# Taking two evicted blocks apart with two VectorE instructions instead of four, in a graph network kernel

## What is computed

```python
def _L0_gnn_ref(node_feats, edge_feats, src, dst, W_e, b_e, eps, W1, b1, gamma, beta, W2, b2):
    e = edge_feats @ W_e + b_e
    m = jax.nn.relu(e + node_feats[src])
    agg = jax.ops.segment_sum(m, dst, num_segments=n)
    h = agg + (1.0 + eps) * node_feats
    z = h @ W1 + b1
    ...                                  # batch norm, relu
    return z @ W2 + b2

def gcn_layer(h, W, b):                  # three of them, each with relu
    hw = h @ W
    msg = hw[src] * norm[:, None]        # norm from the degrees, self loops included
    return jax.ops.segment_sum(msg, dst, num_segments=n) + b

x = _layernorm(x + _L0_gnn_ref(x, ...))
x = _layernorm(x + _L1_gnn_ref(x, ...))
```

## Time and profile before

| | |
|---|---|
| runs | 3148.88, 3151.97, 3140.8 us (median 3148.88) |
| profiled execution | 3141.62 us, of which the span from first to last instruction is 3139.8 us |
| TensorE busy | 2557.4 us (81%), granted clock 0.825 of full speed over the span |
| VectorE busy | 2149.1 us (68%) |
| GpSimd busy | 1605.2 us (51%) |
| ScalarE busy | 968.6 us (31%) |

### The profile page before, as it was taken

One profiled execution on the slowest core, in us unless ns is written; L12 is line 12 of the kernel. 1 busy time (PEld: TensorE's weight loads), 2 busy tenths in 40 slices (PEclk: granted clock), 3 DMA queues, 4 the chain that ended last, 5 costly groups with the idle time before them and its releaser, 6 DMA issues.

```text
span 3139.8 us, 48219 instructions
## 1 busy us (share of the span) xinstructions
PE 2557.4 (81%) x16328; PEld 2238.1 (71%) x16328; DVE 2149.1 (68%) x4255; ACT 968.6 (31%) x1165; POOL 1605.2 (51%) x1582
## 2 busy tenths in 40 slices
PE   4767878777778777777778787787899999999995
PEld 4667767677667766767677776666788888888884
DVE  8767677776767676767676777765798854454446
ACT  1112222222222222222222222226555554455441
POOL 7777777777777777777777777740000000000000
PEclk9687777877777777777776777778999999999997
DMA  6444444444444444444444444432334323323332
GB/s 218 113 120 122 125 124 126 119 125 123 124 124 123 126 123 126 123 125 123 125 124 123 123 124 122 126 98 78 124 121 161 141 107 135 157 105 140 141 141 83
DMA packets 145379, 394.65 MB, mean 126 GB/s; under 512 B 36821, under 2 KB 100096, under 8 KB 139760
## 3 DMA queue, kind: packets, MB, share of 16 engines
q1 hardware_dynamic: 93298, 278.01, 24.6%
q0 software_dynamic: 50176, 102.50, 15.3%
q10 hardware_dynamic: 1662, 10.97, 0.9%
HBM read 286.56 MB, written 104.77 MB: 125 GB/s over the span
## 4 chain that ended last, share of the span: by engine, by line
POOL 48%; PE 30%; issue 15%; DVE 3%; ACT 2%; DMA 1%; DVEq 0%; SPq 0%; ACTq 0%
POOL work L662 48%; PE psE L958 13%; PE psA L958 13%; PE psA L929 1%; PE psA L901 1%; PE psS L890 1%; PE psE L823 1%; ACT wide L767 0%; PE psA L851 0%; PE psS L837 0%; DVE z L1200 0%; PE psE L885 0%; DMA work<-in_x_flat,idx 0%; ACT xn L740 0%; PE psA L885 0%
## 5 line engine op out<-in xcount | busy, mean ns | idle before, releaser
L662 POOL DMA_INDIRECT work<-in_x_flat,idx x1568 | 1598.0, 1019 | 485.7 <-issue 476.5
L823 PE MATMUL psE<-we,work 65*128 65x128 f32 x3136 | 594.4, 367 | 471.1 <-DVE work L1086 426.6
L823 PEld LDWEIGHTS psE<-we,work 65*128 65x128 f32 x3136 | 548.2, 271 | 491.0 <-DMA work<-in_edge_cols 377.6
L1086 DVE TENSOR_TENSOR work<-psE,work 128x1024 f32<-128x1024 f32 x196 | 239.9, 1224 | 557.4 <-DMA work<-in_x_flat,idx 556.7
L851 PE MATMUL psA<-z 128*128 128x245 bf16 x3136 | 582.7, 354 | 0.0
L1106 DVE TENSOR_SCALAR z<-iota_c,key,scale 128x490 bf16<-128x490 f16 x1568 | 555.1, 415 | 21.6 <-DVE z L1098 0.9
L700 ACT ACTIVATE work<-psA 128x490 int32 x392 | 227.3, 580 | 903.9 <-PE psA L851 887.6
L958 PE MATMUL psE<-wide,halves 128*128 128x500 f32 (+1 forms) x2058 | 447.9, 375 | 5.7 <-ACT halves L776 5.3
L837 PEld LDWEIGHTS psS<-onehot,work 128*128 128x128 f32 x3136 | 417.1, 214 | 38.5 <-issue 32.8
L837 PE MATMUL psS<-onehot,work 128*128 128x72 f32 x3136 | 419.6, 292 | 21.2 <-DVE acc L1118 21.2
L687 ACT ACTIVATE work<-work 128x1024 f32<-128x1024 f32 x196 | 207.2, 1057 | 733.7 <-DVE work L1086 733.6
(11 more groups left out here) (160 smaller groups left out, 1330.1 us busy)
## 6 DMA issues: line engine op xcount, KB each, us to landing
counts<-adjacency SPq DMA_DIRECT2D x36, 3062.5 KB, 9.9
adjacency<-work SPq DMA_DIRECT2D x392, 245.0 KB
work<-in_edge_cols SPq DMA_DIRECT2D x196, 256.0 KB
work<-in_x_flat,idx POOLq DMA_INDIRECT x1568
counts<-adjacency SPq DMA_DIRECT2D x3, 1592.5 KB, 6.2
acc<-in_x_cols ACTq DMA_DIRECT2D x1, 3136.0 KB, 23.2
xn<-in_x_rows ACTq DMA_DIRECT2D x1, 3136.0 KB, 32.0
x_spill<-xn SPq DMA_DIRECT2D x12, 256.0 KB, 2.3
```

Of the source, the lines that this page charges most:

```text
L662: gp.indirect_dma_start(gath[0:size(g), g % R, j, :], None, x_flat[:, :], bass.IndirectOffsetOnAxis(ap=idx[0:size(g), g, j:j + 1], axis=0) ...
L823: mm = pe.matmul(psE0[0:n, j, :], eaT[0:FE + 1, g % RE, j, 0:n], we[:, :], start=True, stop=True)
L1086: ve.tensor_tensor(gath[0:n, g % R, :, :], psE0[0:n, :, :], gath[0:n, g % R, :, :], ALU.add).then_inc(sum_ok, 1)
```

## The change

Four changes go together. VectorE takes both banks of a step apart with two instructions on 980 values each, where it used four on 490. Both stand behind `add_window`; the first bank's used to stand ahead of `low_hots`. The semaphore that releases the stored blocks to SyncE, and the buffers to ScalarE, now rises by two after the second instruction. There are four stored blocks instead of three, and the work area grows by 490 words a partition.

```diff
-SLOTS = 3
+SLOTS = 4
...
-        work = sb("work", [P, 9574])
+        work = sb("work", [P, 10064])
...
-            def take_apart(w):
-                ve.wait_ge(evac_ok, w + 1)
+            def take_apart(s):
+                w = HQ * s
+                ve.wait_ge(evac_ok, w + HQ)
                 if w >= SLOTS:
-                    ve.wait_ge(stored[w % SLOTS], 16 * (w // SLOTS))
-                to, fro = full[:, w % SLOTS, :, :, :], taken_low[:, w % TAKEN, :, :]
+                    for i in range(HQ):
+                        ve.wait_ge(stored[(w + i) % SLOTS], 16 * ((w + i) // SLOTS))
+                to = full[:, w % SLOTS:w % SLOTS + HQ, :, :, :].rearrange("p s b h n -> p (s b) h n")
+                fro = taken_low[:, w % TAKEN:w % TAKEN + HQ, :, :].rearrange("p s b n -> p (s b) n")
                 ve.tensor_scalar(to[:, :, 0, :], fro, NIBBLES, None, ALU.bitwise_and)
-                ve.tensor_scalar(to[:, :, 1, :], fro, 4, NIBBLES, ALU.logical_shift_right, ALU.bitwise_and).then_inc(apart_ok, 1)
+                ve.tensor_scalar(to[:, :, 1, :], fro, 4, NIBBLES, ALU.logical_shift_right, ALU.bitwise_and).then_inc(apart_ok, HQ)
...
                     window_hot(s + 1)
-                    if s >= 1:
-                        take_apart(2 * (s - 1))
                     low_hots(s + 1)
...
                 add_window(s, at)
                 if s >= 1:
-                    if s + 1 == G:
-                        take_apart(2 * (s - 1))
-                    take_apart(2 * (s - 1) + 1)
+                    take_apart(s - 1)
...
-            for m in range(2 * (G - 1), 2 * G):
-                take_apart(m)
+            take_apart(G - 1)
```

More of the change, by code:

```diff
@@ L183, in build @@
         taken_low = taken.bitcast(U16).rearrange("p s (b n two) -> p s b n two", b=2, two=2)[:, :, :, :, 0]
-        assert taken_at + TAKEN * 2 * HC <= 9574 and RB * HC + LB * J * P // 2 <= 10112
+        assert taken_at + TAKEN * 2 * HC <= 10064 and RB * HC + LB * J * P // 2 <= 10112
         wide_at = dead_at
```

## The result

| | before | after |
|---|---|---|
| median | 3145.68 us (3138.53 to 3151.97, 13 runs) | 3156.13 us (3150.38 to 3161.58, 13 runs) |
| span of the profiled execution | 3139.8 us | 3156.1 us |
| VectorE busy | 2149.1 us, 4255 instructions | 2132.5 us, 3863 instructions |
| granted TensorE clock over the span | 0.825 | 0.822 |

The ratio is 1.0035, with a 95% interval from 1.0025 to 1.0045: the changed kernel is slower by 10.4 us. VectorE works 17 us less and the kernel takes longer. The forecast was 3,197 us, slower by 48 to 55. The direction was right and the size was not.

What follows compares the result with a forecast made beforehand. GpSimd's gather issues were taken as the bound; waits for VectorE would add 0.24 to 0.33 us a step, taken as 55 us on 3,141.6: 3,197 us. Likeliest case 3,165 to 3,225; 8 in 10 for 3,110 to 3,280.

Steps and rivals of the forecast that it cites:

- What bounds: Graph stage: eight GpSimd gather issues set a step of 10.51 us, 0.52 us of it waits caused by VectorE.
- No change: Rival: only VectorE's busy time moves and gathers lose 0.5 us as before; 3,142 to 3,149 us, chance 0.13.
- L: Time from the end of a group's last gather issue to T; forecast to fall from 3.3 towards 1.6 to 2.5 us.
- T: Start of the row addition L1086, from which all VectorE work of a step follows at fixed distances.
- The long pair's durations: The two VectorE instructions on 980 values: each 0.58 us of VectorE's time, 0.65 us from start to end.
- The wait at L1098 or L1092: Gather requests held by VectorE: at L = 1.8, 0.63 us at L1098 and 0.07 at the first long instruction.
- 0.12 (L1106): Gather request held until a running L1106 ends: 0.12 us a step at L = 1.6 and 2.5.
- 0.40 (second long instruction): Gather request held until the second 980-value instruction ends: 0.40 us a step at L = 1.6 and 2.5.
- the sum: Waits added per step: 10.75 us against 10.42 (regular) to 10.51 (mean), 46 to 64 us in 193 steps.
- one every 0.32: Spacing of the four L1106 in VectorE's step: ends from T + 4.19 to 5.16 before, 3.54 to 4.51 after.
- Longer waits: Rival: L rests at 1.6, requests wait longer, step 11.09 us, 120 us more in all: 3,262 us, chance 0.17.
- The port rule: VectorE in two-port mode and GpSimd share ports; first issuer keeps them, so twice the length waits up to twice as long.

Runs made afterwards that it cites:

- early load: The changed kernel with the edge load issued between the two stores instead of behind them: 3178.73 us, ratio 1.0114.
- the place alone: The kernel before with four stored blocks and four instructions on 490 values, both pairs behind the window addition: 3187.47 us, ratio 1.0134.
- the first order: The changed kernel with VectorE's step reordered, window addition first, then L1092, and no gap behind low_hots: 3352.11 us, ratio 1.0661.
- early pair: The changed kernel with its two 980-value instructions ahead of low_hots instead of behind the window addition (also called length): 3154.6 us, ratio 1.0019.
- slots: The kernel before with only the fourth stored block and the larger work area: 3148.29 us, ratio 0.9997.
- no gap: The changed kernel with TensorE instead of VectorE waiting for low_hots, removing 0.11 us of VectorE idle time behind it: 3269.37 us, ratio 1.0391.
- second order: The changed kernel with VectorE's step reordered, two L1106 and a long instruction first, add_window late, wait behind low_hots kept: 3223.19 us, ratio 1.0238.

## Why the prediction was right in sign and wrong in size

**What bounds: right.** GpSimd's issues bound before and after. VectorE's saving (17 us busy) found no place in the chain, and "No change" by unchanged waits is not what happened either.

**L: right.** "L falls from 3.3 towards 1.6 to 2.5": 1.65. The stores were forecast at T + 6.33 and 8.6 to 9.6, the load at 9.0 to 10.0; they leave at T + 6.4, 9.0 and 9.4 (medians). The early load shows the mechanism from the other side.

**The long pair's durations: nearly right.** 0.65 us forecast; L1117 takes 0.651, L1116 0.864. In the early place L1116 takes 0.676. Behind the window addition an issue has begun 0.6 us ahead of it (1009.36), and the same extra 0.2 us stood in the L1113 of 0.61 behind L1118 in the earlier trace rows: I had carried it into the distances, not into the duration. GpSimd seems to hold VectorE up there in turn; no run tested that.

**The wait at L1098 or L1092: right.** Forecast for L = 1.8 were 0.63 and 0.07; the median waits at L = 1.8 are 0.61 and 0.05. At the usual L of 1.65 they are 0.55 and 0.05.

**The step that failed: what else is held up.** The prediction let a running L1106 hold a request until its end, and so added 0.12 (L1106) and with it 0.40 (second long instruction) at L = 1.6 and 2.5. These are not there. The longest wait of a request met by each instruction, from all issues of the traces of before, after, the place alone and the first order (requests that were passed over, below, left out):

| instruction | length us | longest wait us |
|---|---|---|
| L1106 (490 values) | 0.40 | 0.13 |
| L1113, L1114 (490 values) | 0.40 | 0.26 |
| L1116, L1117 (980 values) | 0.65 | 0.47 |
| L1092 | 0.75 | 0.59 |
| L1098 | 1.22 | 1.07 |
| L1086, L1118 or L1121 | 1.23, 0.29 | 0 |

L1106 holds a request up only in its last 0.13 us. But that alone doesn't take the 0.12 away. The request came at T + 4.39, just where the sum had it, and the sum had the fourth L1106 end at T + 4.51, 0.12 later. In the steps with L = 1.6 that end is at T + 4.7 and the third L1106's at T + 4.38. The second L1106, behind a request let in at T + 3.14, lasts 0.61 us there, and 0.5 in most other steps, where the earlier trace rows had already shown four L1106 in 1.45 us and not in the 1.37 of "one every 0.32". So the request came 0.3 us ahead of an end, where an L1106 holds nobody: of the 170 requests that came at T + 4.2 to 4.5 in the changed kernel, 169 waited for nothing. Nor did the sum keep to its own rule: at L = 1.8 and 3.3 it has a request at T + 4.27 and charges nothing, though the fourth L1106 would be running.

The steps with L = 1.5 to 1.7 took 10.59 us (median), not 11.09, and those at 2.5 took 10.24, not 10.74. "Longer waits", at 3,262 us, rested on the same term. The 0.40 at L1117 hung on it too: only a request that an L1106 had delayed would have come late enough to be held up by L1117.

**The sum.** "0.24 to 0.33 us, in 193 steps 46 to 64". The regular step rose by 0.19, where 0.33 was forecast: 10.75 (for L of 1.8 to 2.5) against a measured 10.59, at an L of 1.65 for which the forecast's own row of holds would have said 11.1. The mean rose by 0.07, where 0.24 was. That second term failed by its form: I compared a forecast *regular* step with the *mean* of before, and the mean holds 18 steps of over 10.9 us that the new order leaves out (6 remain). In 15 of the 18 a request asked at T + 3.14, behind a wait at L1092, and lost 0.54 at L1098; now L1098 ends at T + 3.02. Mean against mean, 10.585 less 10.51 in 193 steps is 14 us, what the last gather's start shows. That the forecast came no further off is in part luck: with the L that came, 1.65, its own rule gives the 3,262 us of "Longer waits".

**The port rule: half right.** The Trainium skill (SBUF — State Buffer, "Who interferes with whom") says of VectorE instructions in a two-port mode that who issues first keeps the shared port pair for the whole instruction. L1092 and L1098 are TENSOR_TENSOR instructions and by the same section have no such mode, so they are no evidence for it. This case's rows agree in the main for the 980-value pair (0.47 of 0.65 us), and the step from 0.26 to 0.47 is as the rule would have it; they do not for L1106, 0.13 of 0.40. And L1092 and L1098 hold requests up too, for 0.59 of 0.75 and 1.07 of 1.22 us. The measurement decides.

## What to carry to other kernels

An engine that waits several microseconds a step for data can still set the pace of another, by when its instructions lie; ask of a re-ordering what it does to the phase, and which transfers it moves ahead of or behind the ones that the phase hangs on. Test the parts of a change one by one: here a free one, one of +6 us and one of +42 us made +10. And when a forecast says "per step", compare medians with medians or means with means: the disturbed steps are part of what a change moves.

## What the runs showed of the hardware

- **A landing depends on what was issued just ahead.** The same gather's rows were there 1.65 us after its issue (median, changed kernel) or 3.0 to 3.25 us (before, early load, early pair). Over 170 steps in each of ten traces (before, changed twice, slots, place, length, early load, no gap, both orders) the edge load had gone out before that gather's issue had ended in 907, with a median L of 3.18, and behind it in 793. In 663 of these no store had gone out in the 0.1 to 1.0 us ahead of that end, and L was 1.65; in the other 130 one had, and L was 2.1 (but 1.64 in the first order's 25). So the load does most of it, and a store alone at times a part.
- **A request can be passed over.** In a few places of before an issue lasts 3.28 us. It began as the row addition ended, and was let in at L1098's end, past L1092 and both short instructions:

```profile
1703.44 1.21 DVE L1086 TENSOR_TENSOR work<-psE,work 128x1024 f32<-128x1024 f32 x1
1704.57 0.74 DVE L1092 TENSOR_TENSOR onehot<-rel,iota_w 128x576 f32<-128x576 f32 x1
1704.64 3.28 POOL L662 DMA_INDIRECT work<-in_x_flat,idx  x1 [0.30 <-issue]
```

  In the two kernels without a gap it happens in most steps, in the second order in 48 of 170 (waits of 0.3 to 2.4 us in all). In before, the kernel without a gap and nearly all of these steps of the second order the request came within 0.13 us of a change from one VectorE instruction to the next; in the first order it often came in the middle of `low_hots`, so that is not the whole of it. What chooses between the first and a later end was not settled.
- **0.11 us of VectorE's idle time was worth some 110 us**, by the phase: taking the wait behind `low_hots` away did VectorE's work earlier and the kernel's later.
